# Gating y on GpSimd instead of VectorE in a fused Mamba and mixture-of-experts layer

## The reference, cut to what matters

```python
xz = layernorm(x) @ in_proj_w.T;  x_, z = split(xz)
xc = silu(causal_conv4(x_))
dt_r, Bc, Cc = split(xc @ x_proj_w.T)
delta = softplus(dt_r @ dt_proj_w.T + dt_proj_bias)
# per token t:  h = h * exp(delta_t * A) + (delta_t * xc_t) * B_t ;  y_t = sum_n h * C_t
y = y + xc * D_param
y = y * silu(z)                      # the gating that the change moves
x = x + y @ out_proj_w.T
x = x + moe(layernorm(x))            # top 2 of 8 experts, silu(h w1) * (h w3), then w2
```

## Time and profile before

| | |
|---|---|
| median of three runs | 4508.96 us (4506.35 to 4510.2) |
| the profiled execution's own time | 4514.08 us |
| its span | 4512.3 us |
| mean granted clock of PE | 0.96 of full speed |
| busy over the span | PE 91%, DVE 54%, ACT 43%, POOL 41% |
| mixer | from the start to about 2440 us |
| experts | the rest |

### The profile page before, as it was taken

One profiled execution on the slowest core, in us unless ns is written; L12 is line 12 of the kernel. 1 busy time (PEld: TensorE's weight loads), 2 busy tenths in 40 slices (PEclk: granted clock), 3 DMA queues, 4 the chain that ended last, 5 costly groups with the idle time before them and its releaser, 6 DMA issues. The chain is left out here.

```text
span 4512.3 us, 70361 instructions
## 1 busy us (share of the span) xinstructions
PE 4108.5 (91%) x25764; PEld 3335.3 (74%) x25764; DVE 2422.2 (54%) x3217; ACT 1940.5 (43%) x4097; POOL 1854.3 (41%) x1396
## 2 busy tenths in 40 slices
PE   6687889989899989889974999999999999999998
PEld 5565677767777777767763888888888888888887
DVE  5999999999999999999993000000000000000000
ACT  7677777877777777778660000000000000000000
POOL 3667777887688777877862000000000000000000
PEclk8888999999999999999986999999999999999999
DMA  4111445354545454555433203030300303030300
GB/s 154 61 61 66 144 163 164 117 172 156 171 121 159 159 176 120 159 165 172 138 106 117 61 14 112 15 112 14 112 14 14 112 14 112 14 111 16 112 14 12
DMA packets 289343, 451.99 MB, mean 100 GB/s; under 512 B 15862, under 2 KB 183414, under 8 KB 280822
## 3 DMA queue, kind: packets, MB, share of 16 engines
q1 hardware_dynamic: 272358, 412.21, 28.0%
q0 software_dynamic: 14768, 34.41, 4.1%
q10 hardware_dynamic: 2016, 2.86, 0.2%
HBM read 920.96 MB, written 45.95 MB: 214 GB/s over the span
## 5 line engine op out<-in xcount | busy, mean ns | idle before, releaser
L576 POOL TENSOR_TENSOR hs<-hs,bc 128x1024 f32<-128x1024 f32 x512 | 1214.2, 2372 | 304.8 <-DVE hs L1264 282.7
L1264 DVE TENSOR_TENSOR_SCAN hs<-dA,pU 128x1024 f32<-128x1024 f32 x512 | 1169.1, 2283 | 46.2 <-ACT dA L694 24.1
L1746 ACT ACTIVATE gate<-pA 128x512 f32<-128x512 f32 x216 | 117.4, 544 | 1861.1 <-PE pB L1788 1861.1
L1661 POOL DMA_INDIRECT out<-ow,trow x54 | 83.5, 1547 | 1972.9 <-DVE ow L1883 1972.9
L694 ACT ACTIVATE dA<-delta,aneg 128x255 f32<-128x255 f32 x2048 | 852.6, 518 | 37.4 <-DVE hs L1264 34.6
L1788 PE MATMUL pA<-xT,w1s 128*128 128x128 f32 x6048 | 800.6, 275 | 0.7 <-ACT xT L1759 0.7
L1788 PE MATMUL pB<-xT,w3s 128*128 128x128 f32 x6048 | 800.0, 275 | 0.0
L1063 PE MATMUL pY<-ident,hs 128*128 128x128 f32 x4096 | 566.7, 286 | 240.6 <-POOL hs L576 240.6
L1788 PEld LDWEIGHTS pA<-xT,w1s 128*128 128x128 f32 x6048 | 741.8, 192 | 26.4 <-issue 25.4
L1063 PEld LDWEIGHTS pY<-ident,hs 128*128 128x128 f32 x4096 | 489.1, 147 | 347.2 <-POOL hs L576 170.3
L1788 PEld LDWEIGHTS pB<-xT,w3s 128*128 128x128 f32 x6048 | 737.4, 192 | 0.0
(11 more groups left out here) (271 smaller groups left out, 3606.8 us busy)
## 6 DMA issues: line engine op xcount, KB each, us to landing
w1s<-in_w SPq DMA_DIRECT2D x165, 1024.0 KB
w3s<-in_w SPq DMA_DIRECT2D x165, 1024.0 KB
w2s<-in_w SPq DMA_DIRECT2D x165, 1024.0 KB
ew<-in_w SPq DMA_DIRECT2D x273, 512.0 KB, 4.1
win<-in_w_in SPq DMA_DIRECT2D x128, 512.0 KB, 4.7
bc<-bc_d SPq DMA_DIRECT2D x64, 1024.0 KB
w1s<-in_w SPq DMA_DIRECT2D x55, 512.0 KB
w3s<-in_w SPq DMA_DIRECT2D x55, 512.0 KB
```

What stands on the lines that cost most here:

```text
L576: pool.tensor_tensor(hs[b][:, :, :], hs[b][:, :, :], bc[:, N + g * PN:N + (g + 1) * PN, :], ALU.mult)\
L1264: dve.tensor_tensor_scan(hs[b][:, :, :].rearrange("p n t -> p (n t)"), dA[b][:, :, :].rearrange("p n t -> p (n t)"), pU[:, :, :].rearrange ...
L1746: act.activation(gate[q % 2][:, 0:n, :], pA[q % 2][:, 0:n, :], ACT.Silu).then_inc(silu, 1)
```

## The change

`finish` moves from DVE to POOL. POOL can't read the turned y where it stands, in PSUM, so ACT copies it into `ysum` first (`copy_back`), one slot behind `copy_y`. The places are: on POOL, chunks 0 to 5 behind the `weigh` of pieces 8, 12, 16, 20, 24, 28, chunk 6 and 7 behind pieces 0 and 5 of the next step; on ACT, slots 3, 5, ..., 15, and slot 1 of the next step for chunk 7. PE's bank is free on ACT's copy (`y_back`), `ysum` on POOL's product (`gated`). The second half of the output product for t=0 moves from slot 2 to slot 3.

```diff
-        OUT_SLOTS = (1, 2, 4, 5)
+        OUT_SLOTS = (1, 3, 4, 5)
...
+            def finish(n, c, nodd):                      # GpSimd
+                ge(pool, y_back, CH * n + c + 1)
+                ge(pool, z_ready, n + 1)
+                pool.tensor_tensor(sz[nodd][:, c, :], ysum[c % 2][:, :], sz[nodd][:, c, :], ALU.mult).then_inc(gated, 1)
...
                     if scan:
                         weigh(s, odd, i)
+                    if back and i == 0:
+                        finish(s - 1, CH - 2, fodd)
+                    if back and i == 5:
+                        finish(s - 1, CH - 1, fodd)
+                    if scan and i % PPC == 0 and i >= 2 * PPC:
+                        finish(s, i // PPC - 2, odd)
                     if i == 1 and s >= 2:
                         for t in range(TT):
                             scatter(s - 2, 1, t)
...
                 def copy_y(n, c):
                     ge(act, summed, PIECES * n + PPC * (c + 1))
-                    ge(act, y_turned, CH * n + c - 1)
+                    ge(act, gated, CH * n + c - 1)
                     act.activation(ysum[c % 2][:, :], pY[c % 2][:, 0:T], ACT.Copy).then_inc(y_copied, 1)
+
+                def copy_back(n, c):
+                    ge(act, y_turned, CH * n + c + 1)
+                    act.activation(ysum[c % 2][:, :], pY[c % 2][:, T:2 * T], ACT.Copy).then_inc(y_back, 1)
...
+                    if u == 1 and back:
+                        copy_back(r, CH - 1)
+                    if scan and u % UPC == 1 and u > UPC:
+                        copy_back(s, u // UPC - 1)
                     rest(u)
...
                     if g == 0:
-                        ge(pe, gated, CH * s + c - 1)
+                        ge(pe, y_back, CH * s + c - 1)
...
-                def finish(n, c, nodd):                      # VectorE
-                    ge(dve, y_turned, CH * n + c + 1)
-                    ge(dve, z_ready, n + 1)
-                    dve.tensor_tensor(sz[nodd][:, c, :], pY[c % 2][:, T:2 * T], sz[nodd][:, c, :], ALU.mult).then_inc(gated, 1)
...
-                    if scan and u % UPC == 0 and c >= 2 and g == 2:
-                        finish(s, c - 2, odd)
-                    if back and at == (0, 0):
-                        finish(r, CH - 2, fodd)
-                    if back and at == (2, 0):
-                        finish(r, CH - 1, fodd)
```

More of the change, by code:

```diff
@@ L243, in mixer @@
         y_turned = sem("y_turned")
+        y_back = sem("y_back")
         gated = sem("gated")
```

## The result

The kernel became slower: 4534.45 us (median of 4 runs, 4531.77 to 4538.82) against 4509.58 (4506.35 to 4510.79) beside it, ratio 1.0059 with a 95% interval of 1.0046 to 1.0071. That is +24.9 us where +19.5 was forecast. The rows explain the 18.0.

What follows compares the result with a forecast made beforehand. Bound in even tile steps by POOL's delay, passed through PE to DVE; DVE paces steps 0 to 3 and 15. Terms -3.9 + 14.4 + 3.0 + 2.1 + 3.9 = +19.5 us on 4508.96 gave 4528.5, range 4503 to 4545.

Steps and rivals of the forecast that it cites:

- What bounds the kernel: Even tile steps: POOL's delay between pieces 1 and 14 reaches the step's end whole, by PE, then DVE.
- What DVE gets back: Each product taken off DVE saves 0.17 us where DVE paces; steps 0, 1, 3 and 15 together -3.9 us.
- ACT's copies: Slot 11's copy delays PE's router product by 0.27 us in the 11 tile steps that PE ends.
- POOL in even tile steps: Three products of 0.72 us while POOL is full, plus ACT's 0.27: +2.4 us, six times, +14.4.
- POOL in odd tile steps: Piece 5's product delays a `weigh` and DVE's feed: +0.9 us in steps 5, 7, +0.4 in 9, 11, 13; +3.0 together.
- Step 2: DVE waits uncovered at `residual(0)` for the moved half: +3.0 us, less five savings, +2.1.
- The tail: After step 15, `finish` of chunk 7 stands behind `add_rows` and delays the last halves: +3.9 us.
- The output product in slot 3: Half done later, after a 3.6 us projection; DVE waits 4.3 us at `residual(0)`, covered by 5.2 in even tile steps.
- DVE doesn't pace: Denies the rival that DVE paces everywhere and all 128 savings count: 4491 us, or 4459 at full 0.42; chance 0.09.
- The port as price of everything: Rival: through the shared SBUF port DVE loses all that POOL gains, +71 us, 4580; chance 0.02.
- Gains and losses: Rival: they meet, POOL's products passing only in part, 0.7 of 2.4 us; +6 us, 4515, no change; chance 0.21.
- The paid wait at `residual(0)`: Rival: even steps pay DVE's 4.3 us wait, odd ones 1.5; +35 us, 4544, much slower; chance 0.15.

Runs made afterwards that it cites:

- e2: Kernel before plus ACT's copies and unused POOL products in the change's places, DVE still gating, half in slot 2: 4525.89 us, ratio 1.0038.
- e9: Changed kernel with PE's turning of y repeated to fill idle time, for chunk 0 (four or three times) and chunk 2 (three times): 4529.08 us, ratio 1.0049.
- e4: Kernel before plus only ACT's copies of the turned y; DVE still gates from PSUM, POOL does nothing new: 4511.06 us, ratio 1.0009.
- e6: Kernel before with the half moved to slot 3 and PE's idle time there filled by turning chunk 0's y four or three times: 4516.99 us, ratio 1.0017.
- e1: Kernel before with only the output product's second half for t=0 moved from slot 2 to slot 3: 4529.06 us, ratio 1.0045.
- e3: Changed kernel with the half back in slot 2 and POOL's product for chunk 7 behind piece 3 instead of 5: 4521.30 us, ratio 1.0035.
- e5: Changed kernel with PE's idle time in slot 3 filled by turning chunk 0's y four or three times: 4541.64 us, ratio 1.0062.
- e10: Kernel before with POOL gating only in steps 0, 1, 2 and 15, and chunk 2's y turned three times in steps 4 to 14: 4505.06 us, ratio 0.9997.
- e8: Kernel before with POOL gating, from ACT's copies, only in steps 0, 1, 2 and 15; DVE gates elsewhere, half in slot 2: 4503.78 us, ratio 0.9992.

## Why the prediction was right

The direction, the mechanism and most terms held; the size came out 5 us low, and one step failed: the price of the projection ahead of the moved half. Between the two profiles the terms of the sum make 21.8 us for 19.5 forecast; the other -3.8 are the lead-in and the expert part, for which it had no term. By its own steps:

- **What bounds the kernel**: right. POOL's load reaches the end of the even step, by PE. With overtime taken off, even steps are 2.0 us longer in e2 and 2.2 in e9, for 2.4 forecast.
- **What DVE gets back**: right in the sum, not in its parts. Steps 0, 1, 3 and 15 were to give 0.9 to 1.1 each, -3.9. 0, 1 and 15 gave -4.1; step 3 had a low-clock stretch in this profile and gave -0.3 in the changed kernel's second one. Inflow and scan are 1.53 us apart.
- **ACT's copies**: right. 0.27 a step reckoned; e4 shows 0.3 in even steps, with the wait of 0.16 us at the router product, and nothing in odd steps without overtime. The prediction names 11 tile steps that PE ends and then has DVE end three of them; its sum goes by the second.
- **POOL in even tile steps**: +14.4 forecast, +17.7 measured. The term was right less overtime (2.4 a step, and 2.2 in e9) and lacked the clock: the even steps have 8.3 us of overtime after and 5.2 before.
- **POOL in odd tile steps**: +3.0 forecast, +3.0 in the sum. The feed's lock was read rightly. That the five evened out so well is luck: less overtime they are 0.9 longer each, not 0.6, of which some 0.3 is the measure's own error; and before had overtime in steps 5 and 7, after in 13, with a slow projection in slot 3 on top.
- **Step 2**: +2.1 forecast, 0.05 measured. The wait came; that a feed would no longer meet a `weigh` was not looked for.
- **The tail**: +3.9 forecast, 3.5.
- **The output product in slot 3** has the step that failed: "does the fourth x projection, 3.6 us as in the earlier trace rows". It takes 4.9 to 5.3 us in four of the six even tile steps and in one odd one. What was missed is on the engine from which the half was taken. The half had filled PE's time until the `weigh` of piece 5; without it PE idles 3 us there, and then often runs at 1.2 GHz for part of the projection. The earlier trace rows held the warning, a projection of 5.38 us behind 2.76 of idle time. The sentence "In even tile steps that is covered" holds: e6 shows the cover eat 4.3 us whole. Alone, the move cost 22.5 us (e1), of which 15 go when the gap is filled (e6, in different comparisons). Beside the gating it is worth ten to nineteen (e3 against the two measurements of the change), where the forecast had 2.1 in step 2 and some two of the tail's 3.9. But there the slow projection of an even step reaches hardly further than POOL's delay, and most of the rest is overtime behind PE's last wait. That this overtime comes from the moved half is not shown: e5 fills the gap and has more of it.
- **The rivals**: DVE doesn't pace the tile steps, for e3 gives it all savings and the half its old slot and is still 14.7 us slower. The port as price of everything is out: 1.27 against 0.44 us is the lock, on one feed in an odd step, while inflows and scans keep their 1.23 and 2.29. Gains and losses don't meet: POOL's products pass nearly whole, 1.9 us at PE's last wait in e2 for 2.16 forecast. The paid wait at `residual(0)` named the right place and a wrong mechanism: 5.9 us in four of the six even steps is 4.2 and a slow projection.

What stays open: why a low-clock stretch falls into one step and not into the next of the same program. Filling gaps lowered the overtime in e6 and e9, raised it behind the last wait in e5, and did nothing in e10. A rival cause was not tried: PE's wait for weights in slot 13, behind which all overtime of the kernel before stands, is filled in no run. The changed kernel's own overtime was 12.0 us in one profile and 22.5 in another, and its distance to the kernel before went from 24.9 to 33.3. That the overtime is what separates those two is likely by their spans, and not shown by an experiment.

## What to carry to other kernels

An operation on the busiest engine is worth what its neighbours leave uncovered, here 0.17 of 0.42 us; on an engine that is behind it costs nearly its full duration (three products and a copy, 2.4 us, made a step 2.0 to 2.4 longer), and whoever is passed the lead inherits it. So ask of each stage who is behind in it, and give work to GpSimd only where that isn't GpSimd (in e8 four steps gained 5.5 us together). Before moving work out of a slot of TensorE, look at what it would otherwise wait for there: an idle stretch that costs nothing by itself can be followed by matmuls at half the clock. And compare steps at the same granted clock before reading a difference of a us or two.

## What the runs showed of the hardware

- Sixteen matmuls of a projection took 3.62 us at a granted clock of 1.00, and 5.30 to 5.39 at 0.67 to 0.68. Such a stretch costs these matmuls 1.7 us; each of the tile steps 3 to 14 of the kernels run here had none to three of them behind PE's last wait for GpSimd.
- A low-clock stretch came behind 3.0 and 2.6 us of idle time (after, e1), but also behind 13 us in which TensorE was busy for 12.0 (e5). And none came behind 2.9 and 2.7 us in steps 6 and 10 of the changed kernel.
- A two-operand GpSimd product took 0.72 to 0.74 us in most places, 0.91 where it began during VectorE's feed in step 8 (0.91 to 0.93 in all six even tile steps) and 1.33 where it began under the end of `add_rows`, an indirect DMA, in the tail.
